# Attention on one core: the next step's projection chunk behind the value products in PE's order

## The reference

```python
x = L0_attn_queries                       # (4, 1024, 256)
xn = _layernorm(x, axis=-1)
x = x + attention(xn, Wq, Wkv, Wout, bout) + ffn(xn, w_gate, w_up, w_down)

# attention: 16 heads of 64
q, k, v = xn @ Wq, *split(xn @ Wkv)       # split into heads
q, k = rope(q), rope(k)                   # the first 32 of 64 dims turn
attn = softmax(einsum('bhid,bhjd->bhij', q, k) * 64 ** -0.5)
out = einsum('bhij,bhjd->bhid', attn, v)
return out @ Wout + bout

# ffn: both linears with blockwise FP4 quantised inputs and weights
return fp4_linear(silu(fp4_linear(x, w_gate)) * fp4_linear(x, w_up), w_down)
```

## Time and profile before

| | us |
|---|---|
| median of 3 runs | 1833.71 (1833.51 to 1835.2) |
| profiled execution | 1836.2 |
| its span | 1834.4 |
| PE busy | 1759.2 (96%) |
| PEld busy | 1088.1 (59%) |
| DVE busy | 1447.7 (79%) |
| ACT busy | 1066.0 (58%) |
| POOL busy | 1394.4 (76%) |

### The profile page before, as it was taken

How to read it: one execution, slowest core, us unless ns; L and a number is a source line. 1 busy time by engine, 2 the same in 40 slices (tenths; PEclk the granted TensorE clock), 3 DMA queues, 4 the chain that set the end, 5 groups by cost and what they waited for, 6 DMA issues and landing times.

```text
span 1834.4 us, 29198 instructions
## 1 busy us (share of the span) xinstructions
PE 1759.2 (96%) x10596; PEld 1088.1 (59%) x10596; DVE 1447.7 (79%) x2034; ACT 1066.0 (58%) x1334; POOL 1394.4 (76%) x688
## 2 busy tenths in 40 slices
PE   6979999968999999999999999999999999999899
PEld 4768999944555555555555555555555555554499
DVE  7978999978878887888788778888787878786263
ACT  4643333315666766676666666666666666767541
POOL 3863544414899899999998989999989899999810
PEclk9999999988999999999999999999999999999899
DMA  8651131121223253333234332233343323322594
GB/s 288 242 199 46 63 116 35 50 72 46 73 79 96 80 151 82 85 91 86 86 90 131 97 90 85 88 85 91 103 117 81 106 79 85 91 82 67 162 322 138
DMA packets 164591, 195.11 MB, mean 106 GB/s; under 512 B 48352, under 2 KB 112736, under 8 KB 164192
## 3 DMA queue, kind: packets, MB, share of 16 engines
q1 hardware_dynamic: 164448, 193.25, 33.9%
HBM read 133.69 MB, written 59.51 MB: 105 GB/s over the span
## 4 chain that ended last, share of the span: by engine, by line
PE 67%; DVE 19%; issue 4%; POOL 1%; DMA 1%; ACT 0%; SPq 0%; DVEq 0%; POOLq 0%; ACTq 0%
PE banks L1025 19%; PE banks L1003 17%; PE banks L945 11%; PE banks L979 9%; PE banks L1578 5%; PE banks L1008 3%; DVE half_max L1069 3%; PE banks L1034 2%; DVE h_scales L110 2%; DVE f_y L131 2%; DVE f_amax L109 2%; DVE f_y L134 2%; DVE h L583 1%; DVE q_lo L1112 1%; DVE f_inv L111 1%
## 5 line engine op out<-in xcount | busy, mean ns | idle before, releaser
L1190 POOL TENSOR_TENSOR acc<-acc,prob 128x1024 f32<-128x1024 f32 x384 | 917.8, 2390 | 80.4 <-ACT prob L1229 48.1
L1069 DVE TENSOR_REDUCE half_max<-banks 128x2 f32<-128x1024 f32 x512 | 627.1, 1226 | 218.3 <-PE banks L979 215.4
L1229 ACT ACTIVATE prob<-banks 128x1024 f32<-128x1024 f32 x512 | 509.6, 1023 | 398.4 <-PE banks L1008 390.5
L1025 PE MATMUL banks<-prob,v 128*64 128x512 f32 x2048 | 497.1, 606 | 0.0
L1241 ACT ACTIVATE banks<-max_all 128x1024 f32<-128x1024 f32 x256 | 263.4, 1029 | 15.3 <-DVE half_max L1069 3.4
L1025 PEld LDWEIGHTS banks<-prob,v 128*64 128x64 f32 x2048 | 124.6, 136 | 228.6 <-issue 190.2
L979 PE MATMUL banks<-k_hi,q_hi 64*128 64x512 f32 x1024 | 232.9, 451 | 17.9 <-DVE half_max L1069 16.3
L979 PEld LDWEIGHTS banks<-k_hi,q_hi 64*128 64x128 f32 x1024 | 96.5, 186 | 233.6 <-issue 125.9
L1190 POOL TENSOR_TENSOR acc<-prob,prob 128x1024 f32<-128x1024 f32 x64 | 153.5, 2399 | 92.7 <-ACT prob L1229 92.7
L945 PE MATMUL banks<-xT,wqk 128*128 128x512 f32 x768 | 217.3, 419 | 2.1 <-DVE k_lo L1112 2.1
L1003 PE MATMUL banks<-q_hi,k_hi 64*128 64x512 f32 x1024 | 204.4, 394 | 9.1 <-ACT prob L1229 9.1
(11 more groups left out here) (121 smaller groups left out, 2145.9 us busy)
## 6 DMA issues: line engine op xcount, KB each, us to landing
max_all<-max_scratch SPq DMA_DIRECT2D x64, 512.0 KB, 4.4
v_scratch<-v_out SPq DMA_DIRECT2D x32, 512.0 KB, 2.6
wqk<-wp_scratch SPq DMA_DIRECT2D x32, 512.0 KB, 3.8
v<-v_scratch SPq DMA_DIRECT2D x32, 512.0 KB, 5.8
inv_rows<-inv_scratch SPq DMA_DIRECT2D x128, 128.0 KB, 3.3
o_scratch<-o_norm SPq DMA_DIRECT2D x64, 256.0 KB, 2.2
o_in<-o_scratch SPq DMA_DIRECT2D x8, 2048.0 KB, 10.4
xn_scratch<-p_xT SPq DMA_DIRECT2D x32, 256.0 KB, 2.9
```

What stands on the lines that cost most here:

```text
L1025: ins = nc.tensor.matmul(o_ps[head * DH:(head + 1) * DH, :], v[s % 2][:, kt, at:at + DH], prob[n % SLOTS][:, head, :], start=kt == 0, stop ...
L1069: nc.vector.tensor_reduce(half_max[:, half % 2, :, t % GRP, part], guess_bank(s, i), axis=AX.X, op=ALU.max, negate=True).then_inc(half_max ...
L1190: nc.gpsimd.tensor_tensor(acc[b][:, :, :], first, prob[n % SLOTS][:, :, :], ALU.add).then_inc(added, 1)
L1229: nc.scalar.activation(prob[n % SLOTS][:, :, :], s_ps[n % 2][:, :, :], ACT.Exp).then_inc(exp_done, 1)
```

## The change

In a round that has a chunk, PE's queue now holds the value products first and the chunk behind them, right ahead of the next round's first guess. Nothing else is changed: the same instructions with the same waits, and no other engine's queue differs.

```diff
                 if scoring(s + 1):
                     guess(s + 1, 2 * r + 1)
-                if r in CHUNK_ROUND and scoring(s + 2) and (s + 2, CHUNK_ROUND[r]) != (0, K0):
-                    project(pe, s + 2, CHUNK_ROUND[r])
                 for n in (s * UNITS + 2 * r - 2, s * UNITS + 2 * r - 1):
                     if 0 <= n < STEPS * UNITS:
                         values(n)
+                if r in CHUNK_ROUND and scoring(s + 2) and (s + 2, CHUNK_ROUND[r]) != (0, K0):
+                    project(pe, s + 2, CHUNK_ROUND[r])
                 if r == 2 and s == STEPS:
```

## The result

| us | before | changed |
|---|---|---|
| median | 1834.45 (1833.51 to 1835.75, 4 runs) | 2005.26 (2002.27 to 2005.88, 4 runs) |
| profiled span | 1834.4 | 2003.6 |

The ratio is 1.0925, with a 95% interval of 1.091 to 1.094: 170.8 us slower. The forecast was 1998.7, the range 1976 to 2038.

What follows compares the result with a forecast made beforehand. PE's queue was taken as the bound. A step loses 2 x 1.40 + 2 x 1.35 = 5.50 us, 30 steps 165.0, giving 1998.7 us from a median of 1833.71; range 1976 to 2038.

Steps and rivals of the forecast that it cites:

- PE bounds the stage, and a new order can only lose there: From 437 to 1657 us PE works 1216.87 of 1220.00 us; a new order could win at most 3.1 us.
- The chunk comes 1.86 later and DVE's slack of 0.46 goes: Chunk behind 8 matmuls, 1.86 us later; DVE's 0.46 between shuffle and the even round's first maximum is used up.
- 1.21 us at the second guess in the rounds with sums, 1.40 at the sums: Rounds 1 to 2 and 5 to 6: PE waits 1.21 us for the first maximum; column sums start 1.40 late.
- 1.35 in the rounds with the turn: Rounds 3 to 4 and 7 to 0, with the turn of the maxima: second guess 1.35 us later.
- The seam at zero: Chunk directly behind value products in PE's queue: no extra cost, 0.09 us either way for the range.
- PE's busy time unchanged: Sign: PE's busy time stays the same while the stage takes 1385 us and a step 46.4 instead of 40.9.
- The load unit's waits near 155 us in all: Sign: load unit waits for the maximum ahead of 120 second guesses, 1.2 to 1.4 us each, near 155 in all.
- The clock stayed at 1.00: Rival: pauses of 1.2 to 1.35 us make PE's clock fall, adding 158 us, some 2157; chance 5%.
- Copy_o did not come into play: Rival: ACT's late copy_o holds up value products asked for 1.59 us earlier, room 0.94; 2059 with one us beyond; chance 4%.
- Both kinds of pause appeared: Rival: only one kind of pause appears, say DVE catches up in turn rounds, leaving 84 us, 1918; chance 3%.
- weight loads pulled ahead of running matmuls: Skill rule: could take up to about 0.19 us off each pause, 22.8 us in all; left out of the sum.
- frequent short pauses: Skill rule: such pauses between groups of matmuls make the clock go up and down; by it the clock rival, 5%, happens.

Runs made afterwards that it cites:

- The 60 places alone: Against the kernel before, only the chunks of rounds 1 and 5 moved behind the value products: 1916.99 us, 81.2 over before.
- the two other orders that I ran: Against the kernel before: chunk between its round's two value products, 1902.37 us; chunk ahead of its round's second guess, 1958.68 us.
- the kernel with the three operations behind the maximum: Changed kernel with DVE's crossed, straight and shuffle behind the next round's first maximum instead of ahead of it: 2076.6 us.

## Why the prediction held

- **PE bounds the stage, and a new order can only lose there.** Confirmed as far as it was tried: 3.1 us idle before, 139.5 after, the work the same, and none of the orders that I ran won anything.
- **The chunk comes 1.86 later and DVE's slack of 0.46 goes.** Confirmed: the first maximum starts right behind the shuffle, 0.63 in the rows above, where I took 0.62 from the earlier trace rows.
- **1.21 us at the second guess in the rounds with sums, 1.40 at the sums.** Measured 1.25 and 1.37. The 60 places alone gave 81.2 us, against 60 x 1.40 = 84.
- **1.35 in the rounds with the turn.** This term was too small, the mechanism was right. The wait itself is 1.38, 0.03 more than forecast. The rest is that I took the value products to follow the guess as they did before. Behind a guess that has waited they start 0.44 later (1016.17, 1016.61), where in such a round it was 0.34 (1025.55, 1025.89). So the place costs 1.47, 0.12 more than forecast, and 60 x 0.12 = 7 us; the rounds with sums give back 60 x 0.03 = 2. These 5 are most of what the loss of 170.8 us is over the forecast 165.0. In the rounds with sums the later start of the value products costs nothing more, since there the low part ends last.
- **The seam at zero.** It was taken without a row that shows it, and it came out right for the order of the change: an odd round takes 1024.21 - 1018.47 = 5.74 of PE's queue, and 1013.06 - 1007.33 = 5.73 before. Wrong as a rule: the two other orders that I ran had seams of 0.16 and 0.20 a round, outside the 0.09 that I had allowed.
- **PE's busy time unchanged.** This sign was wrong: it rose from 1759.2 to 1792.4. A row's end is the end of its last matmul, which otherwise lies under the next row. A pause uncovers it: of the 1.47 us that a turn round loses only 1.20 are told as idle, of the 1.37 of a round with sums 1.09, and 120 times the 0.27 to 0.28 between them are the 33 us by which the busy time rose.
- **The load unit's waits near 155 us in all.** The waits are there, their size was wrong. The load unit has 236.1 us in 179 waits for a maximum, where the kernel before had 48.7 in 60. Each new one is longer than PE's own (1.51 against 1.09 at 1027.42), since the load unit had run ahead of PE and is idle earlier. What counts for the time is PE's pause.
- **The rivals.** The clock stayed at 1.00. Copy_o did not come into play: the waits in the stretch show none on it. Both kinds of pause appeared. The rule that the prediction took from the Trainium skill, "TensorE: Matmul & The Clock Gate", on weight loads pulled ahead of running matmuls took nothing off here: the load starts with its matmul at 1027.42, 0.05 behind the maximum's end (1026.16 + 1.21). The same page's rule in the Trainium skill on frequent short pauses (section "A second HAM failure mode: psum-queue depth-cycling") did not come out in the changed kernel either, with some 120 pauses of up to 1.2 us and the clock at 1.00; in a kernel with longer ones the clock did go down and up, as the last section shows.

What the experiments add is the cause. Two changes that leave PE's order alone, a longer row on DVE and a shorter one, move the time by about what they put in beyond the slack, or by all that they take out; and the pause follows the three operations when these change places.

## What to carry to other kernels

In front of an engine with no idle time, a piece of work may be moved only by as much as the engine that answers it has slack, and that slack is to be read at the answer that is wanted next, which may belong to quite other work: here a maximum that had nothing to do with the chunk but stood behind it in DVE's queue. Beyond the slack, each of the 120 places cost the rest in full. Moving the piece earlier cost here too (122.9 us, against 170.8 for moving it later), and tearing a pair of matmul groups apart cost some 0.16 us a place on top.

## What the runs showed of the hardware

- A dip of the clock behind a wait of some 2 us. In the kernel with the three operations behind the maximum, the stage's clock is 0.99. The end of one round 2 shows where it falls (busy time by stretch, columns as above):

```profile
1036.00:1038.00 2.00, 0.17 (x2) 0.00 (x0) 2.00 (x3) 1.56 (x3) 0.90 (x2) 1.00 0.03 10
...
1040.00:1042.00 2.00, 2.00 (x12) 1.18 (x8) 0.48 (x1) 1.24 (x2) 2.00 (x3) 0.50 0.02 6
```

  PE stood nearly still from 1036 to 1038, and from 1040 to 1042, when it was busy again, it had the lower level, 1.2 GHz. The matmuls there are slower:

```profile
1039.28 0.40 PE L1003 MATMUL banks<-q_lo,k_hi 64*128 64x512 f32 x2
...
1040.67 0.64 PE L1003 MATMUL banks<-q_lo,k_hi 64*128 64x512 f32 x2
```

  This round takes 5.70 us from its first guess to its chunk (1038.71 to 1044.41), the like round before it 4.15 (1014.55 to 1018.70), so 1.55 more. By the trace's record of the granted clock that happens nine times behind such a wait of 1.97 to 2.00 us, though the wait comes some 60 times; what picks out the nine is not shown. A tenth dip stands at the stage's start, from 442 to 446, behind a pause of 3.16 us. 9 x 1.55 = 14 of the 17 us that were left, an estimate from one round.
- Groups of matmuls have seams of some 0.1 us that depend on the neighbour and that no row names. From a guess to the value products it is 0.32 to 0.34 if the guess runs right behind scores (1015.02, 1015.34; 1025.55, 1025.89). It is 0.43 to 0.44 if the guess has waited (1016.17, 1016.61), and also if it has not waited but follows the chunk (1008.16, 1008.59, with the chunk ahead of the guess).
- On DVE, an operation that waits for the end of the one right before it starts 0.73 behind it in the rows read: the shuffle behind crossed where straight is left out (1009.79, 1010.52), and the repeated products of DVE's longer row (1.45 for two). Straight, which waits for nothing, starts 0.61 behind crossed (1024.32, 1024.93 in the changed kernel).
